# Windowed attention with top-1 experts on one core: where the second group's rows are turned, rounded and routed

## The reference

```
q, k, v = x @ w{q,k,v}.T + b            # 16 heads of 16
scores  = q k / 4 inside each window of 128 rows, 0 elsewhere,
          plus q k / 4 among the 64 global rows (every 32nd) of a batch
attn    = softmax(scores over all 2048) @ v
x = layernorm(x + attn @ wo.T + bo)
top1 = argmax(x @ Wg.T)                 # of 8 experts
xhat = (x - mean) * rsqrt(var + 1e-5)
y    = gelu((xhat*s_e + b_e) @ W1_e + b1_e) @ W2_e + b2_e   for e = top1
out  = layernorm(x + y)
```

## Time and profile before

| | us |
|---|---|
| median of 3 runs (449.38 to 451.81) | 451.41 |
| the profiled execution, its own time | 451.29 |
| its span | 449.5 |
| PE busy | 408.3 (91%) |
| DVE busy | 333.3 (74%) |
| ACT busy | 248.8 (55%) |
| POOL busy | 220.5 (49%) |

### The profile page before, as it was taken

How to read it: one execution, slowest core, us unless ns; L and a number is a source line. 1 busy time by engine, 2 the same in 40 slices (tenths; PEclk the granted TensorE clock), 3 DMA queues, 4 the chain that set the end, 5 groups by cost and what they waited for, 6 DMA issues and landing times.

```text
span 449.5 us, 14666 instructions
## 1 busy us (share of the span) xinstructions
PE 408.3 (91%) x5747; PEld 342.6 (76%) x5747; DVE 333.3 (74%) x809; ACT 248.8 (55%) x519; POOL 220.5 (49%) x301
## 2 busy tenths in 40 slices
PE   5889889999999999999999999889799999989952
PEld 4758778888888888888888788767487877868852
DVE  7795677757757757767769987563578899899884
ACT  3415665665665665765765765866555555643410
POOL 5341343463463464454554674544544458556650
PEclk9999999999999999999999999999799999999998
DMA  8653740000000000000020000000000011101112
GB/s 248 184 184 107 235 140 2 27 25 0 23 23 0 23 23 1 23 23 3 20 72 25 2 4 3 1 2 1 1 1 1 1 50 47 47 0 47 48 47 93
DMA packets 21704, 20.34 MB, mean 45 GB/s; under 512 B 3117, under 2 KB 21666, under 8 KB 21666
## 3 DMA queue, kind: packets, MB, share of 16 engines
q1 hardware_dynamic: 17428, 15.60, 11.0%
q10 hardware_dynamic: 4238, 4.22, 2.9%
HBM read 15.41 MB, written 4.41 MB: 44 GB/s over the span
## 4 chain that ended last, share of the span: by engine, by line
PE 53%; DVE 29%; issue 8%; ACT 8%; DVEq 0%; POOL 0%; ACTq 0%; POOLq 0%
DVE row_max_t L1140 10%; PE ps L1435 8%; PE ps L1398 7%; PE ps L1711 6%; PE ps L1536 5%; PE ps L1358 5%; PE ps L1389 5%; PE ps L1412 3%; PE ps L1418 3%; DVE k_part L998 2%; ACT probs L841 2%; PE ps L1380 2%; ACT boundsT_t L852 2%; ACT k_part L707 2%; PE ps L1402 2%
## 5 line engine op out<-in xcount | busy, mean ns | idle before, releaser
L841 ACT ACTIVATE probs<-ps 128x1024 f32<-128x1024 f32 x64 | 62.1, 1022 | 68.6 <-PE ps L1402 68.6
L1140 DVE TENSOR_REDUCE row_max_t<-ps 128x16 f32<-128x2048 f32 x31 | 70.9, 2288 | 3.8 <-PE ps L1389 3.5
L1711 PE MATMUL ps<-w_part,hm_part 128*128 128x256 f32 x384 | 56.0, 296 | 7.0 <-DVE ysum L1294 5.1
L1711 PEld LDWEIGHTS ps<-w_part,hm_part 128*128 128x128 f32 x384 | 50.2, 197 | 10.1 <-DVE ysum L1294 5.3
L1389 PE MATMUL ps<-k_part,q_part 32*128 32x128 f32 x1584 | 51.5, 274 | 3.1 <-issue 1.3
L1389 PEld LDWEIGHTS ps<-k_part,q_part 32*128 32x128 f32 x1584 | 47.0, 186 | 9.2 <-issue 7.0
L557 POOL TENSOR_TENSOR q_part<-qf,q_part 128x512 fp32r<-128x512 f32 x32 | 41.0, 1283 | 26.1 <-ACT q_part L689 26.1
L1536 PE MATMUL ps<-xh_parts,w_part 128*128 128x512 f32 x192 | 53.7, 416 | 0.0
L599 POOL TENSOR_TENSOR attn_t<-num_t,rden_t 128x256 f32<-128x256 f32 x32 | 19.9, 623 | 65.2 <-DVE rden_t L1171 65.2
L782 ACT ACTIVATE ffn_rows<-ps,b1s 128x512 f32<-128x512 f32 x32 | 22.0, 687 | 42.7 <-PE ps L1536 34.6
L1398 PE MATMUL ps<-q_part,k_part 32*128 32x256 f32 x768 | 35.6, 294 | 4.5 <-DVE row_max_t L1140 3.4
(11 more groups left out here) (231 smaller groups left out, 925.4 us busy)
## 6 DMA issues: line engine op xcount, KB each, us to landing
table<-rest_sums SPq DMA_DIRECT2D x4, 1088.0 KB, 6.2
xs<-in_L_attn_x_dram SPq DMA_DIRECT2D x16, 256.0 KB, 2.7
rows<-in_L_attn_x_dram ACTq DMA_DIRECT2D x4, 1024.0 KB, 7.5
out_dram<-yout SPq DMA_DIRECT2D x7, 512.0 KB, 2.9
w<-in_L_ffn_W_dram SPq DMA_DIRECT2D x2, 256.0 KB, 8.2
w<-in_L_ffn_W_dram SPq DMA_DIRECT2D x1, 512.0 KB, 3.9
out_dram<-yout SPq DMA_DIRECT2D x2, 256.0 KB, 2.2
w_raw<-in_L_attn_wq_dram SPq DMA_DIRECT2D x1, 256.0 KB, 2.8
```

The costliest lines, as they stand in the source:

```text
L841: act.activation(probs[:, 2 * h:2 * h + 2, :], ps[:, 2 * h:2 * h + 2, :], ACT.Exp).then_inc(probs_ready, 1)
L1140: dve.tensor_reduce(row_max[:], ps_all, op=ALU.max, axis=AX.X).then_inc(max_ready, 1)
L1711: mm(y, hm_part[a][:, 1 - p, f, c * P:(c + 1) * P], w2_part[b][:, f, :], start=(f == 0 and i == 0), stop=False)
```

## The change

`turn_rows(1)` moves on PE from t = 33 to the end of t = 32, behind `first_layer(0, 0, 0)`; `logits(1)` to the end of t = 33, ahead of `first_layer` c = 2; `turn_logits(1)` ahead of `first_layer` c = 3; `turn_onehot(1)` from t = 35 to right behind it. On ACT `evacuate(1)` moves to t = 33, `keep_logits(1)` to the front of the group work of t = 34, and `keep_onehot(1)` from t = 35 to t = 34, ahead of `scale_rows(2)`. On DVE `take_high(1)` moves to the end of t = 33, and `route` from t = 35 to t = 34, behind the statistics of window 31. POOL and SP keep their order. No instruction is added or taken away.

```diff
--- before.py
+++ after.py
@@ -864,6 +864,8 @@
 
                     act.activation(e_arg[:, 0, :], zeros16[:], ACT.Gelu)
                 if not steady and t == NW + 1:
+                    for pair in range(2):
+                        evacuate(1, 1, pair, False)
                     hidden_high(0, 0, 0)
                     hidden(0, 0, 1)
                     hidden_high(0, 0, 1)
@@ -871,16 +873,14 @@
                     act.wait_ge(ld_w2, 16)
                     copy(w2_part[0][:], w2[:]).then_inc(w2_high_ready, 1)
                 if not steady and t == NW + 2:
-                    for pair in range(2):
-                        evacuate(1, 1, pair, False)
+                    keep_logits(1)
                     hidden(0, 0, 2)
-                    keep_logits(1)
                     hidden_high(0, 0, 2)
+                    keep_onehot(1, 1)
                     for pair in range(2):
                         scale_rows(2, pair)
                 if not steady and t == NW + 3:
                     hidden(0, 0, 3)
-                    keep_onehot(1, 1)
                     hidden_high(0, 0, 3)
 
             attention_steps(act, step, first=0)
@@ -1191,6 +1191,9 @@
                     early(6)
                     dve.wait_ge(residual_ready, t - 2)
                     dve.bn_stats(bn6[:, 1 - p, :], residual[:, 1 - p, :]).then_inc(bn_ready, 1)
+                if not steady and t == NW + 2:
+                    for k in range(ROUTE_STEPS):
+                        route(k, 1)
                 if not steady and t == FACTORS_AT:
                     gate_columns()
                 if not steady and FACTORS_AT < t < FACTORS_AT + 4:
@@ -1209,12 +1212,9 @@
                 if not steady and t == NW:
                     dve.wait_ge(b1_sums_in_psum, 1)
                     dve.tensor_tensor(b1s[:], ps[:, 5, 0:FC], b1[:], ALU.add).then_inc(ffn_w_ready, 1)
-                if not steady and t == NW + 2:
+                if not steady and t == NW + 1:
                     for pair in range(2):
                         take_high(1, 1, pair)
-                if not steady and t == NW + 3:
-                    for k in range(ROUTE_STEPS):
-                        route(k, 1)
 
             def gate_columns():
                 dve.wait_ge(late_const, 9)
@@ -1609,14 +1609,9 @@
                     turn_sums().then_inc(sums_in_psum, 1)
                 if old:
                     output_product(t - 3)
-                if not steady and t == NW + 1:
-                    for pair in range(2):
-                        turn_rows(1, pair)
                 if not steady and t == NW + 2:
-                    logits(1, 1)
+                    turn_logits(1)
                     first_layer(0, 0, 3)
-                    turn_logits(1)
-                if not steady and t == NW + 3:
                     turn_onehot(1)
                 if not steady and t == NW - 1:
                     turn_logits(0)
@@ -1644,7 +1639,10 @@
                 if not steady and t == NW:
                     pe.wait_ge(probs_ready, 2 * NW)
                     first_layer(0, 0, 0)
+                    for pair in range(2):
+                        turn_rows(1, pair)
                 if not steady and t == NW + 1:
+                    logits(1, 1)
                     first_layer(0, 0, 2)
 
             turn_weight(WQ)
```

## The result

| | before | after |
|---|---|---|
| median of 7 runs, us | 451.24 (449.38 to 453.08) | 454.87 (454.36 to 456.25) |
| profiled execution, us | 451.29 | 454.64 |
| its span, us | 449.5 | 452.9 |

The ratio after to before is 1.0088, 95% interval 1.0059 to 1.0117: the kernel became 0.9% slower. The forecast was 453.6 us.

What follows compares the result with a forecast made beforehand. PE was taken to bound the kernel wherever fed. Profiled 451.29 plus a 2.2 us shift of group 1's first layer, the clock's 2.8 us cost unchanged, gave 453.5, or 453.6 against the median; range 450.9 to 455.6 us.

Steps and rivals of the forecast that it cites:

- Bound and dip: PE bounds the kernel where fed; ahead of group 1's one-hot transposes a 2.95 us gap, then slow clock costing 2.8 us.
- Turning rows first: PE, group 1's row transposes ahead of window 31's weighing: 0.9 us only moved, leaving a gap before the attention transposes.
- Logits earlier: PE, logits (0.58 us) ahead of window 31's output product's end: product done at 317.4, 1.5 us later than before.
- POOL beside the route: DVE's route beside POOL's take_low: one wait for a POOL operation, one-hot transposes at 320.45, 0.7 us earlier than before.
- rival D: POOL runs earlier, lines 1110 and 1115 each wait for a half of take_low: onehot at 321.2, 454.4 us; chance 0.20.
- Rival C: DVE's line 1115 in the route is not held by POOL: onehot 0.8 us earlier, 452.8 us; chance 0.18.
- ACT behind the one-hot: ACT's hidden c = 3 waits behind one-hot copy and scaling; PE's group 1 first layer starts at 323.9, shift +2.2 us.
- rival B: Group 1's first layer starts right behind the one-hot, about 321.0, at full clock: 447.9 us; chance 0.04.
- The clock: PE idle 4.3 us against 2.95 around group 1's one-hot, so the clock falls again, costing 2.8 us again.
- Rival A: The clock holds because the one-hot transposes cut PE's idle time into 1.35 and 3.0 us: 450.8 us; chance 0.12.
- later work is PE's own and follows with the shift: Everything behind group 1's first layer moves by the same shift, +2.2 us.

Runs made afterwards that it cites:

- the filled kernel before: Kernel before with 11 extra matmuls nobody reads in PE's 2.95 us idle time ahead of group 1's one-hot transposes; 450.31 us.
- the filled changed kernel: Changed kernel with extra matmuls nobody reads on PE, 8 behind first_layer c = 3 and 11 behind the one-hot transposes; 453.50 us.
- the second experiment: Changed kernel with only POOL's order changed: take_low(1) in step 33, both hidden_low of group 0 in step 34 behind group 1's onehot; 453.43 us.
- the version that keeps what paid: Kernel before with logits(1), take_high(1) and route early, turn_rows(1) in its old place, take_low(1) before hidden_low, scale_rows(2) last on ACT; 448.36 us.

## Why the prediction was right, and where it was off

**Bound and dip.** Right: PE was the bound where it had work, and the dip cost what was read from the earlier trace rows. 2.8 us was forecast, 2.6 and 2.7 were measured on PE (the two filled kernels). One term of it was too small: a quarter with the one-hot matmuls takes 3.9 us at the full clock (3.86, 3.87 and 3.89 where the clock stayed up), not 3.70.

**Turning rows first.** Right in mechanism, and in size up to the one-hot transposes: 0.9 forecast, a gap of 0.89, and transposes 1.0 later with this part alone. What it costs in the end, 1.2 us by the medians, is not traced through by its one profile.

**Logits earlier.** The mechanism was right; the sum was 0.3 us short, in three parts of 0.1. The attention transposes started at 314.30, not 314.2. The logits began 0.34 us behind their start, where the first layer had begun 0.17 behind it. And I took 315.89, where the next matmul began, for the end of the product, which the residual waits for: that end is 0.07 us behind the next start before, and 0.15 here (317.72 against 317.57). So the residual started at 317.82, not 317.5.

**POOL beside the route.** This is the term that was mis-sized. I had line 1110 arrive at 318.8, just ahead of take_low, and priced one wait. It came at 319.06, 0.26 us behind take_low's start at 318.80, and both steps waited, 0.87 and 0.77 us above their own length. That is rival D's outcome and only in part its cause: the casts cost POOL 0.3 us instead of 0.55 (313.53 to 318.80, 5.27 us against 4.95), and DVE was later. One-hot transposes at 321.46 instead of 320.45. By the time, too, rival D's 454.4 us was nearer to the 454.87 than the forecast was. The rule of the Trainium skill (SBUF — State Buffer, Who interferes with whom) that a DVE instruction with two SBUF inputs is held by a GpSimd instruction that reads SBUF, and one with a single SBUF input, outside certain modes, is not, agrees with both steps (1.06 and 1.03 us) and with line 1107 beside them (0.19 us). Rival C, that line 1115 isn't held, has fallen.

**ACT behind the one-hot.** Right: from the start of the one-hot transposes to that of L1536 the forecast had 3.45 us and the profile has 3.36, with a gap of 2.96 where 3.0 was forecast; with the copy put back L1536 starts 0.34 us behind the transposes' start, and the time falls by 3.9 us. The change could not do what it was arranged for (rival B) with this order.

**The clock.** Forecast to fall again at a like price: it fell, and c = 1 came 6.58 us behind the first quarter, 6.34 before. Rival A has fallen for this kernel. But the step "later work is PE's own and follows with the shift" holds in one direction only. A delay passed through in full (+3.1 at the first L1536, +3.2 at group 7's mark). A gain did not: the wait for DVE's onehot took back 0.5 to 1.0 us of it in group 2.

In sum the forecast was 453.6 and 454.87 was measured: 0.9 us of the difference is there at the first L1536 (324.82 against 323.9) and comes from the second wait with the 0.3 us before it. The slow passage behind it was 0.24 us longer (6.58 against 6.34), since more of the slow stretch fell behind the start of L1536.

**Behind the last group.** The stretch from group 7's mark to the end of the span took 31.9 to 33.2 us in the eleven profiled executions. The traces show where the difference arises. These are its ends, the filled kernel before first (columns as in the earlier trace rows), then the one with only the rows' transposes moved:

```profile
434.54 2.93 PE L1716 MATMUL ps<-w_part,hm_part 128*128 128x256 f32 x12 [5.13 <-DVE ysum L1294]
...
437.36 1.69 PE L1716 MATMUL ps<-w_part,hm_part 128*128 128x256 f32 x12
```

```profile
438.00:439.00 1.00, 1.00 (x10) 0.94 (x9) 0.57 (x2) 0.00 (x0) 0.00 (x0) 1.00 0.58 203
```

```profile
436.84 2.93 PE L1710 MATMUL ps<-w_part,hm_part 128*128 128x256 f32 x12 [5.13 <-DVE ysum L1294]
...
439.67 2.91 PE L1710 MATMUL ps<-w_part,hm_part 128*128 128x256 f32 x12
```

```profile
441.00:442.00 1.00, 1.00 (x7) 1.00 (x6) 0.00 (x0) 0.00 (x0) 0.00 (x0) 0.50 0.00 0
```

In all eleven PE stands idle for 5.1 us, 19.2 us behind the mark it goes on at the lower clock, and 22.0 us behind it the last product of twelve matmuls begins. That one takes from 1.69 to 2.91 us, according to when the clock comes back. The stretch less this product is 30.1 to 30.3 us in every one. So the 0.6 us that went behind group 7's mark in the filled changed kernel and the 0.7 with the copy put back lie in this product (2.65 and 2.85 us against 2.07), and so does all but 0.1 of the 1.2 with the transposes moved alone (2.91 against 1.84 in the kernel before). Open is what decides when the clock comes back there, and whether it is tied to the edits; each kernel has one profile. The mean granted clock of a run took values from 0.978 to 0.993.

## What to carry to other kernels

When an operation is moved up in a strict queue, list what is queued behind it and who waits for that: here a 0.6 us copy and 1.7 us of scaling were put ahead of a finished quarter's activation, and with the fall of the clock behind that gap they cost 3.9 us, more than the chain that was shortened could give. POOL, working beside DVE's chain of tiny operations, held each of the two that read two tiles of SBUF for one of its own operations, so the chain's place against that engine's queue has to be read, not only its length. And a gain at the head of a stage is worth only what the next-tightest engine of that stage leaves of it: fill the gap with dummy work first, and see how much arrives at the end. Where single profiles differ by a microsecond, look for the stretch in which they part before the edit is given the credit.

## What was not expected of the hardware

A gap of 2.23 us ahead of the one-hot transposes left the clock up in one profiled execution, while gaps of 2.22 and 1.37 us, with 0.4 us of transposes between, let it fall in another; L1536 of 1.66 and of 2.90 us are the two prices. And the fall does not have to come inside the gap: in the second experiment PE had been at work again for 1.4 us, behind gaps of 0.58 and 2.96 us, when the granted clock fell. A COPY of 2 elements per partition (L1159) took 0.16 or 0.17 us in 28 of its 32 runs in the kernel before, but 1.03 us where it started early in one of POOL's L564, and 1.24 and 1.26 us beside L569 in the second experiment and in the version that keeps what paid, so that the shortest operations pay most.
